# Hard attention over a masked graph: the negated maximum moves from VectorE to GpSimd

## The chip, the cores and the metric

One core of one Trainium2 chip. The metric is the device time of one execution of the whole program in microseconds; the time before is the median of three runs. The profile comes from one further execution with the hardware profiler.

## What is computed

A graph network of four layers over N = 3327 nodes with 256 features and a random adjacency matrix (about 1% of the entries are set). Each layer reads a normalised and rectified x and adds its result to x. The change touches the third layer, the hard attention: eight heads of 32 features, where each node gives one eighth of the value of its best-scoring neighbour. Cut to that layer:

```python
def _L2_gnn_ref(x, adj, WQ, WK, WV, we, be):
    Q = (x @ WQ.T).reshape(n, HEADS, HEAD_DIM).transpose(1, 0, 2)
    K = (x @ WK.T).reshape(n, HEADS, HEAD_DIM).transpose(1, 0, 2)
    V = (x @ WV.T).reshape(n, HEADS, HEAD_DIM).transpose(1, 0, 2)
    energy = Q @ we.T + be
    attn = jnp.einsum('hqd,hkd->hqk', Q, K) * SCALING + energy
    attn = attn + jnp.where(adj > 0, 0.0, -jnp.inf)
    attn = jax.nn.softmax(attn, axis=-1)
    hard = (attn == jnp.max(attn, axis=-1, keepdims=True)).astype(jnp.float32) / HEADS
    out = jnp.einsum('hqk,hkd->hqd', hard, V)
    return out.transpose(1, 0, 2).reshape(n, EMBED)
...
h = jnp.maximum(_layernorm(x, axis=-1), 0.0)
x = x + _L2_gnn_ref(h, adj, L2_gnn_WQ, L2_gnn_WK, L2_gnn_WV, L2_gnn_we, L2_gnn_be)
```

## The kernel before

The nodes are padded to NP = 3328, 26 tiles of 128. The stage in question is `hard_attend` (L1482): for each tile i and each head h it handles one unit g = 8 i + h, 208 in all; below a unit is called a head. The rows of scores are 3328 columns wide and are cut into SCH = 4 steps of SW = 832 columns.

Each engine has its own hand-written queue, and semaphores tie the queues together:

- TensorE computes a step of the scores into one of two PSUM slots (`scores`, L1596, two matmuls of 416 columns), turns the one-hot rows (`transposes_a` L1604, `transposes_b` L1613) and multiplies them with the values (`sums`, L1627, 26 matmuls of 64 columns). Its order is written out: scores of the next heads stand between the transposes and sums of earlier ones. A score step waits until VectorE has finished the step that used its PSUM slot.
- VectorE adds the mask's offset to each step, writes the result S and the step's maximum over the columns to one column of mx (`maxima`, L1699; in the profile this is a custom operation and a short accumulator read). Then `maximum` (L1705) reduces the four columns of mx to their negated maximum nmx. The order is: the steps 1 to 3 of head g, step 0 of head g+1, then `maximum(g)`. S is double, so step 0 of head g waits for the exponential of head g-2 (s_hA) and step 2 for the first GpSimd operation of head g-2 (s_gap).
- ScalarE computes exp(S + nmx) for the first 2048 columns into H (`weights`, L1656), which is one where S is the maximum and zero elsewhere, and copies the transposes of the head before out of PSUM (`evacuate`, L1663 with 1024 and L1665 with 640 columns). Once a tile it takes the result (`take_result`, L1672).
- GpSimd makes the same for the remaining 1280 columns in two operations (`not_hot`): gap = (S + nmx) x a large negative number (L1544), then H = gap clipped to 0 and the code of one (L1549). Beside that it turns the adjacency rows into offsets, in eight pieces of 416 columns a tile (`offsets`, L1538): the table OFF_AT puts two pieces behind each of the heads h = 0, 1, 2 (for the next tile) and h = 7 (for the tile after that). It adds the results to x behind h = 4 and 5 (`add_result`, L1558). At tile 23 it clears rows of the last adjacency buffer once (L1571).

mx and nmx hold two heads each.

Of the kernel before, what the change touches and what calls it, by code (L numbers as in the profile page):

```python
# [17 lines left out]
F32 = mybir.dt.float32  # L18
# [6 lines left out]
ALU = mybir.AluOpType  # L25
ACT = mybir.ActivationFunctionType
AX = mybir.AxisListType

N = 3327
P = 128  # L30
# [1331 lines left out]
SCH = 4  # L1362
# [119 lines left out]
def hard_attend(k, adj_dram, KS, Vhl, be, q_dram):  # L1482


    nc = k.nc
    s_pad, s_nb, s_sc, s_tt, s_mx, s_hA, s_gap, s_hB, s_trA, s_trB, s_evA, s_evB, s_av, s_x, s_res, s_be = (
        k.sem(f"s_h2_{n}") for n in ("pad", "nb", "sc", "tt", "mx", "hA", "gap", "hB", "trA", "trB", "evA", "evB", "av", "x", "res", "be"))
    s_rows = [k.sem(f"s_h2_rows{i}") for i in range(2)]
    s_q = [k.sem(f"s_h2_q{i}") for i in range(2)]
    G = NT * HEADS  # L1490
    CA = TA * 2 * P
    with ExitStack() as c:
# [3 lines left out]
        gap = k.sb(c, "h2_gap", [P, NP - CA], F32)  # L1496
# [2 lines left out]
        HT = k.sb(c, "h2_HT", [P, 2, NP], FP8)  # L1499
        QS = k.sb(c, "h2_QS", [KROWS, 2, HEADS, P], F16)  # L1500
        mx = k.sb(c, "h2_mx", [P, 2, SCH], F32)
        nmx = k.sb(c, "h2_nmx", [P, 2], F32)
        ps = k.ps(c, "h2_ps", [P, 2, 2, CH])
        pT = k.ps(c, "h2_pT", [P, 2, 1024], BF16)
# [3 lines left out]
        @block.sync  # L1508
        def _(sp):
            def load(i):  # L1510
                if i >= 2:
                    sp.wait_ge(s_nb, OFF_PARTS * (i - 1))
                if i < NT - 1:
                    sp.dma_start(rows[:, i % 2, 0:N], adj_dram[i * P:(i + 1) * P, :]).then_inc(s_rows[i % 2], 16)
                else:
                    sp.wait_ge(s_pad, 2)
                    for p0, p1 in LAST_CUTS:
                        sp.dma_start(rows[p0:p1, i % 2, 0:N], adj_dram[i * P + p0:i * P + p1, :]).then_inc(s_rows[i % 2], 16)
                if i >= 2:
                    sp.wait_ge(s_sc, SCH * HEADS * (i - 1))  # L1520
                sp.dma_start(QS[0:3 * HD, i % 2], q_dram[:, :, i * P:(i + 1) * P]).then_inc(s_q[i % 2], 16)

            sp.wait_ge(s_pad, 1)
            for i in range(NT):
                load(i)

        @block.gpsimd
        def _(pool):
            nc.gpsimd.memset(rows[:, :, N:NP], 0).then_inc(s_pad, 1)

            def offsets(i, part):
                c0, c1 = part * NP // OFF_PARTS, (part + 1) * NP // OFF_PARTS
                if part == 0:
                    loads = i // 2 + (1 if i < NT - 1 else len(LAST_CUTS))
                    pool.wait_ge(s_rows[i % 2], 16 * loads)
                    if i >= 2:
                        pool.wait_ge(s_tt, SCH * HEADS * (i - 1))
                nc.gpsimd.tensor_scalar(off[:, i % 2, c0:c1], rows[:, i % 2, c0:c1], -1.0, MASK, ALU.add, ALU.mult).then_inc(s_nb, 1)  # L1538

            def not_hot(g):  # L1540
                pool.wait_ge(s_mx, g + 1)
                if g >= 1:
                    pool.wait_ge(s_hB, g)
                nc.gpsimd.tensor_scalar(gap[:], S[:, g % 2, CA:NP], nmx[:, g % 2:g % 2 + 1], -SHARPER,  # L1544
                                        ALU.add, ALU.mult).then_inc(s_gap, 1)
                pool.wait_ge(s_gap, g + 1)
                if g >= 2:
                    pool.wait_ge(s_trB, g - 1)
                nc.gpsimd.tensor_scalar(H[:, g % 2, CA:NP].bitcast(U8), gap[:], float(FP8_ONE), 0.0,  # L1549
                                        ALU.min, ALU.max).then_inc(s_hB, 1)  # L1550

            def add_result(i, part):
                if part == 0:
                    pool.wait_ge(s_res, i + 1)
                else:
                    pool.wait_ge(s_x, 2 * i + 1)
                xs = k.X[:, i, :].rearrange("p (h d) -> p h d", d=HD)
                nc.gpsimd.tensor_tensor(xs, xs, R[:, :, part, :], ALU.add).then_inc(s_x, 1)  # L1558

            pool.wait_ge(s_pad, 1)  # L1560
            for part in range(OFF_PARTS):
                offsets(0, part)
            offsets(1, 0)
            offsets(1, 1)
            for g in range(G):
                i, h = g // HEADS, g % HEADS
                not_hot(g)
                if i == NT - 3 and h == 0:
                    pool.wait_ge(s_nb, OFF_PARTS * (NT - 2) + 2)
                    pool.wait_ge(s_hB, g + 1)  # L1570
                    nc.gpsimd.memset(rows[96:P, (NT - 1) % 2, :], 0).then_inc(s_pad, 1)  # L1571
                    pool.wait_ge(s_pad, 2)
                if i and h in (ADD_AT, ADD_AT + 1):
                    add_result(i - 1, h - ADD_AT)
                j, parts = OFF_AT[h]
                for part in parts:
                    if 1 <= i + j < NT:
                        offsets(i + j, part)
            add_result(NT - 1, 0)
            add_result(NT - 1, 1)  # L1580
# [103 lines left out]
        @block.vector  # L1684
        def _(dve):
            nc.vector.tensor_copy(QS[3 * HD:KROWS].rearrange("p s h n -> p (s h n)"),
                                  be[3 * HD:KROWS, 3:4].to_broadcast([2, 2 * HEADS * P])).then_inc(s_be, 1)
            two = lambda x: x.rearrange("p (b n) -> p b n", b=2)

            def maxima(g, ch):  # L1690
                i, h = g // HEADS, g % HEADS
                if h == 0 and ch == 0:
                    dve.wait_ge(s_nb, OFF_PARTS * (i + 1))
                if g >= 2 and ch == 0:
                    dve.wait_ge(s_hA, g - 1)
                if g >= 2 and ch == 2:
                    dve.wait_ge(s_gap, g - 1)
                dve.wait_ge(s_sc, g * SCH + ch + 1)
                nc.vector.tensor_tensor_reduce(out=two(S[:, g % 2, ch * SW:(ch + 1) * SW]), in0=ps[:, ch % 2, :, 0:SB],  # L1699
                                               in1=two(off[:, i % 2, ch * SW:(ch + 1) * SW]), scale=SHARP, scalar=-3e38,  # L1700
                                               op0=ALU.add, op1=ALU.max, accum_out=mx[:, g % 2, ch:ch + 1]).then_inc(s_tt, 1)

            def maximum(g):
                dve.wait_ge(s_tt, (g + 1) * SCH)
                nc.vector.tensor_reduce(nmx[:, g % 2:g % 2 + 1], mx[:, g % 2, :], AX.X, ALU.max, negate=True).then_inc(s_mx, 1)  # L1705

            maxima(0, 0)
            for g in range(G):
                for ch in range(1, SCH):
                    maxima(g, ch)  # L1710
                if g + 1 < G:
                    maxima(g + 1, 0)
                maximum(g)


def layer2(k, ap):
    with ExitStack() as c:
        q_dram = k.dram("q_dram", (3 * HD, HEADS, NP), F16)
        KS = k.sb(c, "KS", [KROWS, HEADS, NP], F16)
        be = k.sb(c, "be", [KROWS, 4], F32)  # L1720
        Vhl = k.sb(c, "Vhl", [P, NB2, 2, HEADS, 2 * HD], F16)
        with ExitStack() as c1:
            w = k.sb(c1, "w_hard", [P, 3, 2, KC, D], F16)
            hT = k.sb(c1, "hT2", [P, 2, KC, NP], F16)
            part_of = lambda i: lambda part: w[:, i, part, :, :]
            normalise(k, "n2", hT, [(ap[f"L2_gnn_W{n}"], part_of(i)) for i, n in enumerate("QKV")])
            QT = k.sb(c1, "QT", [P, 2, KC, NP], F16)
            KT = k.sb(c1, "KT", [P, 2, KC, NP], F16)
            hard_project(k, ap, hT, w, QT, KT, KS, Vhl, be, q_dram)
        hard_attend(k, ap["adj"], KS, Vhl, be, q_dram)  # L1730
# [258 lines left out]
```

## Time and profile before

| | |
|---|---|
| median of 3 runs | 2261.28 us (2258.91 to 2265.71) |
| profiled execution | 2261.32 us |
| its span | 2259.6 us |
| VectorE busy over the span | 1891.3 us (84%) |
| TensorE busy over the span | 1995.8 us (88%) |
| ScalarE busy over the span | 1627.9 us (72%) |
| GpSimd busy over the span | 885.3 us (39%) |
| score steps on VectorE (L1699) | 832, 800.0 us, 1021 ns each |
| GpSimd's first operation (L1544) | 208, 277.1 us, 1332 ns each |

The shares over the span are means over very different stages, so they don't say what bounds one of them. The hard attention is read by itself below. PE is TensorE, PEld its weight loads, DVE is VectorE, ACT is ScalarE, POOL is GpSimd. In the rows, `h_S` is the buffer S, `h_nmx` the negated maximum, `h_mx` the four maxima, and so on. Operations on one engine can overlap a little, so the distance from start to start is a better price than the duration.

### The profile page before, as it was taken

The page shows a single profiled execution, that of the slowest core. Times are in us where ns is not written, and L with a number is a line of the kernel's source. Part 1 is how long each engine was busy: PE and PEld are TensorE (multiplying, and loading weights), DVE is VectorE, ACT ScalarE, POOL GpSimd, SP SyncE. Part 2 cuts the span into 40 slices and gives each one's busy share as a digit, 9 for nine tenths or more (in the row PEclk, how much of TensorE's full clock was granted, in tenths as well). Part 3 has the DMA queues.
Part 4 walks back from the last instruction along what each step waited for, and adds up shares of the span by engine and source line. Part 5 has one row for each costly group of instructions (what it writes and reads, how often), then busy time and mean ns, then how long its engine had stood idle before and what let it go on. Part 6 is the DMA issues. An engine that isn't in the chain of part 4 may idle for free. (4 is left out here: it accounts for less than half of the span.)

```text
span 2259.6 us, 58783 instructions
## 1 busy us (share of the span) xinstructions
PE 1995.8 (88%) x23703; PEld 1552.8 (69%) x23703; DVE 1891.3 (84%) x4161; ACT 1627.9 (72%) x1955; POOL 885.3 (39%) x867
## 2 busy tenths in 40 slices
PE   4756999999986799999885999999999999986999
PEld 3546999999984488888643666666666666655544
DVE  5585999999996699988775999999999999985322
ACT  4456999999987576553253999999999999895100
POOL 0020000000000144445233888888888888870000
PEclk9958999999997899999987999999999999997999
DMA  9797121221200356679546111111211111101222
GB/s 314 277 368 314 66 86 66 78 83 60 95 11 6 103 153 170 155 177 200 106 96 183 69 69 63 42 69 69 69 69 67 38 69 69 39 2 52 79 80 69
DMA packets 181870, 240.21 MB, mean 106 GB/s; under 512 B 110484, under 2 KB 148020, under 8 KB 178274
## 3 DMA queue, kind: packets, MB, share of 16 engines
q1 hardware_dynamic: 157201, 208.76, 30.1%
q10 hardware_dynamic: 24400, 27.70, 3.7%
q8 instruction: 188, 3.08, 0.6%
q14 instruction: 81, 0.66, 0.1%
HBM read 160.16 MB, written 47.30 MB: 92 GB/s over the span
## 5 line engine op out<-in xcount | busy, mean ns | idle before, releaser
L1699 DVE CUSTOM_DVE_ANT_0 h_S<-h_ps,h_off 128x832 f32<-128x832 f32 x832 | 800.0, 1021 | 14.2 <-POOL h_off L1538 11.3
L1596 PE MATMUL h_ps<-KS,h_QS 98*128 98x416 f16 x1664 | 441.0, 347 | 81.8 <-DVE h_mx L1699 46.4
L1656 ACT ACTIVATE h_H<-h_S,h_nmx 128x2048 fp8e4<-128x2048 f32 x208 | 416.7, 2003 | 81.3 <-DVE h_nmx L1705 81.3
L834 ACT ACTIVATE b_CA<-b_el,HC 128x1152 fp8e4<-128x1152 f32 (+1 forms) x384 | 435.5, 1219 | 3.5 <-DMA b_el<-el_dram 3.5
L931 PE MATMUL b_pb<-b_x,b_B 128*128 128x132 f16 x5408 | 414.3, 221 | 3.9 <-DVE b_B L896 3.4
L931 PEld LDWEIGHTS b_pb<-b_x,b_B 128*128 128x128 fp8e4 x5408 | 340.3, 96 | 6.7 <-DVE b_B L896 6.2
L1544 POOL TENSOR_SCALAR h_gap<-h_S,h_nmx 128x1280 f32<-128x1280 f32 x208 | 277.1, 1332 | 90.0 <-DVE h_nmx L1705 80.8
L912 PE MATMUL b_pz<-b_x,adjT 128*128 128x134 f16 x2704 | 256.6, 221 | 16.4 <-DMA b_x<-xv_dram 16.4
L1549 POOL TENSOR_SCALAR h_H<-h_gap 128x1280 uint8<-128x1280 f32 x208 | 260.5, 1252 | 17.1
L1627 PEld LDWEIGHTS h_po<-Vhl,h_HT 128*128 128x128 fp8e4 x5408 | 215.1, 98 | 65.0 <-ACT h_HT L1663 0.7
L1596 PEld LDWEIGHTS h_ps<-KS,h_QS 98*128 98x128 f16 x1664 | 95.6, 97 | 199.9 <-DVE h_mx L1699 121.9
L1154 POOL MEMSET c_shift<- 128x1 f32 x1 | 0.1, 98 | 591.4 <-POOLq L963 591.4
L1162 POOL TENSOR_SCALAR c_MK<-c_ad 128x512 f16<-128x512 uint8 x169 | 155.1, 918 | 188.3 <-DVE c_V L1263 142.2
L1627 PE MATMUL h_po<-Vhl,h_HT 128*128 128x64 f16 x5408 | 226.2, 193 | 0.6 <-ACT h_HT L1665 0.6
L1663 ACT ACTIVATE h_HT<-h_pT 128x1024 uint16<-128x1024 uint16 x208 | 209.3, 1006 | 0.2 <-PE h_pT L1604 0.2
L849 DVE TENSOR_SCALAR b_CD<-b_el,HC 128x1152 uint8<-128x1152 f32 (+1 forms) x240 | 195.9, 816 | 8.1 <-DMA b_el<-el_dram 8.1
L912 PEld LDWEIGHTS b_pz<-b_x,adjT 128*128 128x128 fp8e4 x2704 | 183.0, 96 | 16.6 <-DMA b_x<-xv_dram 16.6
L1321 PE MATMUL c_pa<-WHhi,c_V 128*128 128x257 f16 x676 | 185.6, 275 | 0.3 <-DVE c_V L1263 0.2
L1323 PE MATMUL c_pa<-WHhi,c_V 128*128 128x257 f16 x676 | 184.7, 273 | 0.0
L896 DVE TENSOR_TENSOR b_B<-b_CA,adjT 128x288 int32<-128x288 int32 (+1 forms) x384 | 170.2, 470 | 17.2 <-ACT b_CA L834 17.0
L1322 PE MATMUL c_pa<-WHlo,c_V 128*128 128x256 f16 x676 | 184.0, 272 | 0.0
L1892 PE MATMUL m_pa<-m_P,m_ad 128*128 128x512 f16 x676 | 154.4, 380 | 0.3 <-DVE m_P L1924 0.3
(208 smaller groups left out, 3245.4 us busy)
## 6 DMA issues: line engine op xcount, KB each, us to landing
h_rows<-in_adj_dram SPq DMA_DIRECT2D x25, 1663.5 KB, 8.1
b_x<-xv_dram SPq DMA_DIRECT2D x48, 435.5 KB, 5.3
s_rows<-in_adj_dram SPq DMA_DIRECT2D x25, 832.0 KB, 7.1
s_rows<-in_adj_dram SPq DMA_DIRECT2D x25, 831.5 KB, 7.6
e_dram<-c_U ACTq DMA_DIRECT2D x78, 256.0 KB, 2.7
adjT_dram<-adjT SPq DMA_DIRECT2D x1, 10816.0 KB, 38.3
c_ad<-adjT_dram SPq DMA_DIRECT2D x13, 832.0 KB, 6.9
m_ad<-adjT_dram SPq DMA_DIRECT2D x13, 832.0 KB, 4.6
```

The lines of the kernel that those rows point to most:

```text
L834: nc.scalar.activation(dst[:, 0:cols], elr[:, n % 2, 0:cols], ACT.Sigmoid, bias=HC[:, h, 1, jt:jt + 1], scale=STEP, saturate=False).then_i ...
L849: nc.vector.tensor_scalar(dst[:, 0:gn * P].bitcast(U8), elr[:, n % 2, 0:gn * P], HC[:, h, 0, jt:jt + 1], float(FP8_ONE), ALU.is_gt, ALU.mu ...
L912: last = nc.tensor.matmul(pz[:, z % 2, r * WZ:(r + 1) * WZ].rearrange("p (h d) -> p h d", h=2), k.adjT[:, g0 + 3 * b + r, jt, :], xb[:, m ...
L931: last = nc.tensor.matmul(pb[:, p, b, r * W:(r + 1) * W].rearrange("p (f d) -> p f d", f=2), B[:, u % RING_B, t * P:(t + 1) * P], xb[:, m ...
L1321: nc.tensor.matmul(pa[:, q, t, 0:D + 1], hi, WHhi[:, jt, :], start=first, stop=False, skip_group_check=True)
L1544: nc.gpsimd.tensor_scalar(gap[:], S[:, g % 2, CA:NP], nmx[:, g % 2:g % 2 + 1], -SHARPER, ALU.add, ALU.mult).then_inc(s_gap, 1)
L1549: nc.gpsimd.tensor_scalar(H[:, g % 2, CA:NP].bitcast(U8), gap[:], float(FP8_ONE), 0.0, ALU.min, ALU.max).then_inc(s_hB, 1)
L1596: last = nc.tensor.matmul(ps[:, ch % 2, b, 0:SB], QS[:, i % 2, h, :], KS[:, h, c0:c0 + SB], start=True, stop=True)
L1627: last = nc.tensor.matmul(po[:, i % 2, h * 2 * HD:(h + 1) * 2 * HD], wt[:, b, :, e], Vhl[:, b, e, h, :], start=(b == 0 and e == 0), stop=( ...
L1656: nc.scalar.activation(H[:, g % 2, 0:CA], S[:, g % 2, 0:CA], ACT.Exp, bias=nmx[:, g % 2:g % 2 + 1], scale=1.0, saturate=False).then_inc(s_ ...
L1663: nc.scalar.activation(HT[:, g % 2, 0:CA].bitcast(U16), pT[:, 0, :].bitcast(U16), ACT.Copy).then_inc(s_evA, 1)
L1699: nc.vector.tensor_tensor_reduce(out=two(S[:, g % 2, ch * SW:(ch + 1) * SW]), in0=ps[:, ch % 2, :, 0:SB], in1=two(off[:, i % 2, ch * SW:(c ...
```

## The change

The semaphore s_top and a buffer `top` of two columns are added. GpSimd forms the negated maximum in two operations of one column each: `first_maxima` takes the largest of the first three maxima once three steps are done, `maximum` takes the larger of that and the fourth and multiplies by -1. Both stand ahead of `not_hot(g)` in GpSimd's queue. VectorE's queue holds the four steps of each head in plain order and nothing else. All that waited for s_mx (the exponential on ScalarE and the first operation of `not_hot`) now waits for GpSimd's second operation.

```diff
@@ hard_attend
+        top = k.sb(c, "h2_top", [P, 2], F32)
@@ gpsimd
+            def first_maxima(g):
+                q = g % 2
+                pool.wait_ge(s_tt, g * SCH + 3)
+                nc.gpsimd.tensor_scalar(top[:, q:q + 1], mx[:, q, 0:1], mx[:, q, 1:2], mx[:, q, 2:3], ALU.max, ALU.max).then_inc(s_top, 1)
+
+            def maximum(g):
+                q = g % 2
+                pool.wait_ge(s_tt, (g + 1) * SCH)
+                pool.wait_ge(s_top, g + 1)
+                nc.gpsimd.tensor_scalar(nmx[:, q:q + 1], top[:, q:q + 1], mx[:, q, 3:4], -1.0, ALU.max, ALU.mult).then_inc(s_mx, 1)
+
@@
             for g in range(G):
                 i, h = g // HEADS, g % HEADS
+                first_maxima(g)
+                maximum(g)
                 not_hot(g)
@@ vector
-            def maximum(g):
-                dve.wait_ge(s_tt, (g + 1) * SCH)
-                nc.vector.tensor_reduce(nmx[:, g % 2:g % 2 + 1], mx[:, g % 2, :], AX.X, ALU.max, negate=True).then_inc(s_mx, 1)
-
-            maxima(0, 0)
             for g in range(G):
-                for ch in range(1, SCH):
+                for ch in range(SCH):
                     maxima(g, ch)
-                if g + 1 < G:
-                    maxima(g + 1, 0)
-                maximum(g)
```

## Rows read from the trace of the kernel before

**Rows 1.** Busy time by stretch: us, then each engine's busy us (instructions), granted clock, DMA
```profile
core 0: us, PE busy (x) PEld busy (x) DVE busy (x) ACT busy (x) POOL busy (x), PEclk, DMA share, GB/s
...
1320.00:1420.00 100.00, 92.67 (x1227) 62.16 (x1224) 100.00 (x237) 92.28 (x81) 86.28 (x86) 1.00 0.18 62
1420.00:1520.00 100.00, 92.48 (x1224) 62.01 (x1222) 99.87 (x235) 92.36 (x82) 85.88 (x85) 1.00 0.17 59
...
1820.00:1920.00 100.00, 92.67 (x1224) 62.18 (x1224) 100.00 (x236) 92.66 (x83) 85.81 (x85) 1.00 0.17 59
```

**Rows 2.** The reduction's line: count, ns min/median/max, first and last start
```profile
L1705 DVE TENSOR_REDUCE h_nmx<-h_mx x208: 152/154/157, 1227.0 to 2025.2; 128x1 f32<-128x4 f32 x104
```

**Rows 3.** Waits from 1300 to 2010 us: who waited for whom, total, times, longest
```profile
PEld h_ps L1596 <- DVE h_mx L1699: 99.0, 346, 0.4
POOL h_gap L1544 <- DVE h_nmx L1705: 65.5, 96, 1.3
ACT h_H L1656 <- DVE h_nmx L1705: 55.9, 162, 2.1
...
PEld h_pT L1613 <- POOL h_H L1549: 2.0, 1, 2.0
DVE h_S L1699 <- PE h_ps L1596: 1.8, 3, 1.1
```

**Rows 4.** VectorE in order of time: start, us, instruction
```profile
1504.77 1.02 DVE L1699 CUSTOM_DVE_ANT_0 h_S<-h_ps,h_off 128x832 f32<-128x832 f32 x1
...
1505.71 1.02 DVE L1699 CUSTOM_DVE_ANT_0 h_S<-h_ps,h_off 128x832 f32<-128x832 f32 x1
...
1507.60 1.02 DVE L1699 CUSTOM_DVE_ANT_0 h_S<-h_ps,h_off 128x832 f32<-128x832 f32 x1
...
1508.55 0.15 DVE L1705 TENSOR_REDUCE h_nmx<-h_mx 128x1 f32<-128x4 f32 x1
1508.61 1.02 DVE L1699 CUSTOM_DVE_ANT_0 h_S<-h_ps,h_off 128x832 f32<-128x832 f32 x1
```

**Rows 5.** GpSimd in order of time, idle time and releaser in brackets
```profile
1505.11 1.33 POOL L1544 TENSOR_SCALAR h_gap<-h_S,h_nmx 128x1280 f32<-128x1280 f32 x1
1506.52 1.25 POOL L1549 TENSOR_SCALAR h_H<-h_gap 128x1280 uint8<-128x1280 f32 x1
1507.86 1.16 POOL L1538 TENSOR_SCALAR h_off<-h_rows 128x416 f32<-128x416 int32 x2
1509.11 1.33 POOL L1544 TENSOR_SCALAR h_gap<-h_S,h_nmx 128x1280 f32<-128x1280 f32 x1
...
1520.32 1.33 POOL L1544 TENSOR_SCALAR h_gap<-h_S,h_nmx 128x1280 f32<-128x1280 f32 x1 [0.56 <-DVE h_nmx L1705]
1521.74 1.25 POOL L1549 TENSOR_SCALAR h_H<-h_gap 128x1280 uint8<-128x1280 f32 x1
1522.95 0.73 POOL L1558 TENSOR_TENSOR X<-X,h_R 128x256 f32<-128x256 f32 x1
1524.17 1.33 POOL L1544 TENSOR_SCALAR h_gap<-h_S,h_nmx 128x1280 f32<-128x1280 f32 x1 [0.49 <-DVE h_nmx L1705]
```

**Rows 6.** GpSimd's groups by shape: count, busy us, mean ns, idle before
```profile
L1544 POOL TENSOR_SCALAR h_gap<-h_S,h_nmx 128x1280 f32<-128x1280 f32 x208 | 277.1, 1332 | 90.0 <-DVE h_nmx L1705 80.8 <-POOL h_H L1549 0.2
L1549 POOL TENSOR_SCALAR h_H<-h_gap 128x1280 uint8<-128x1280 f32 x208 | 260.5, 1252 | 17.1
...
L1538 POOL TENSOR_SCALAR h_off<-h_rows 128x416 f32<-128x416 int32 x208 | 111.8, 537 | 24.5 <-DMA h_rows<-in_adj_dram 8.1
...
L372 POOL TENSOR_SCALAR_AFFINE_SELECT s_corner_f<-s_ones_pp 128x128 f32<-128x128 f32 x1 | 0.3, 283 | 0.3 <-POOL s_rows L369 0.3
...
L1154 POOL MEMSET c_shift<- 128x1 f32 x1 | 0.1, 98 | 591.4 <-POOLq L963 591.4
```

**Rows 7.** GpSimd at the start of the stage, eight offset pieces in a row
```profile
1217.16 4.85 POOL L1538 TENSOR_SCALAR h_off<-h_rows 128x416 f32<-128x416 int32 x8 [7.56 <-DMA h_rows<-in_adj_dram]
```

**Rows 8.** ScalarE's exponential in order of time, idle before it in brackets
```profile
1504.89 2.00 ACT L1656 ACTIVATE h_H<-h_S,h_nmx 128x2048 fp8e4<-128x2048 f32 x1 [0.34 <-DVE h_nmx L1705]
```

**Rows 9.** TensorE: two windows with granted clock, and score matmuls at either clock
```profile
660.00:670.00 10.00, 7.42 (x107) 6.00 (x105) 10.00 (x26) 9.99 (x11) 0.00 (x0) 1.00 0.00 0
...
1225.00:1230.00 5.00, 4.35 (x10) 0.65 (x10) 4.98 (x12) 2.00 (x1) 2.58 (x2) 0.50 0.53 226
...
1218.31 0.14 PEld L1596 LDWEIGHTS h_ps<-KS,h_QS 98*128 98x128 f16 x2 [18.90 <-issue]
...
1231.68 0.90 PE L1596 MATMUL h_ps<-KS,h_QS 98*128 98x416 f16 x2
...
1504.85 0.53 PE L1596 MATMUL h_ps<-KS,h_QS 98*128 98x416 f16 x2
```

More of the change, by code:

```diff
@@ L1485, in hard_attend @@
     nc = k.nc
-    s_pad, s_nb, s_sc, s_tt, s_mx, s_hA, s_gap, s_hB, s_trA, s_trB, s_evA, s_evB, s_av, s_x, s_res, s_be = (
-        k.sem(f"s_h2_{n}") for n in ("pad", "nb", "sc", "tt", "mx", "hA", "gap", "hB", "trA", "trB", "evA", "evB", "av", "x", "res", "be"))
+    s_pad, s_nb, s_sc, s_tt, s_mx, s_hA, s_gap, s_hB, s_trA, s_trB, s_evA, s_evB, s_av, s_x, s_res, s_be, s_top = (
+        k.sem(f"s_h2_{n}") for n in ("pad", "nb", "sc", "tt", "mx", "hA", "gap", "hB", "trA", "trB", "evA", "evB", "av", "x", "res", "be", "top"))
     s_rows = [k.sem(f"s_h2_rows{i}") for i in range(2)]
```

## The prediction

> **What bounds the kernel now.** I began with the busy time by stretch [rows 1]. Between 1320 and 1920 us the kernel does one thing, the hard attention, and there VectorE is busy 99.9 to 100% of the time, TensorE 92%, ScalarE 92% and GpSimd 86%. The reader should see two things: VectorE has no air, and GpSimd has only 14%. The stage is long: the reduction that the change removes runs 208 times, once for each head of each of 26 tiles, from 1227.0 to 2025.2 us [rows 2], 35% of the span.
>
> Next come the waits of the stage [rows 3]. VectorE waited 1.8 us for TensorE in 710 us; everybody else waits for VectorE. TensorE waits for the maxima in 346 cases (weight loads), ScalarE's exponential waits 55.9 us for the negated maximum, GpSimd's first operation 65.5 us. So VectorE's queue sets the pace.
>
> VectorE's instructions in order of time [rows 4] give that pace. Steps start at 1504.77 and 1505.71, 0.94 us apart, although each lasts 1.02 (they overlap). Only the step behind the reduction starts later: the reduction starts at 1508.55 with the end of the step of 1507.60, and the next step at 1508.61, 1.01 behind its predecessor. One head is 1508.61 - 1504.77 = 3.84 us, a tile of eight heads 30.74 (26 of them are 799 us).
>
> GpSimd's instructions in order of time [rows 5] are the view that decides this case. A head with two pieces of the offset runs gap 1505.11, H 1506.52, two pieces from 1507.86, next gap 1509.11: 4.00 us without idle time, more than VectorE's 3.84. Four heads of a tile are like this (h = 7, 0, 1, 2), and GpSimd falls behind in them; it catches up in the others, where gap waits 0.56 or 0.49 us for the maximum. Being late harms nobody now, since ScalarE gets the maximum from VectorE.
>
> **Part 1, what leaves VectorE.** The reduction lasts 0.154 us [rows 2], but overlaps the next step; what it costs is 1.01 - 0.94 = 0.067 us a head [rows 4]. With VectorE alone the head would take 3.777 us, a tile 30.22, and 208 heads would save 208 x 0.067 = 14 us. That is all the change can win at the bound. The new order also gives the maximum of a head without waiting for the next head's first step, up to 0.94 us earlier; this shortens a latency once, at the start of the stage, not the pace.
>
> **Part 2, what arrives at GpSimd.** Per head two single-column operations. The first waits for the third step, the second for the fourth step and for the first; gap waits for the second, and behind it in GpSimd's queue stand H, the offset pieces and the residual additions, then the next head. ScalarE's exponential now waits for GpSimd too, so GpSimd's lateness becomes everybody's.
>
> GpSimd's own work per tile before [rows 5]: 4 offset heads x 4.00 = 16.00. A plain head is 1.41 (gap to H) + 1.25 (H) + 0.08 (the distance that GpSimd keeps behind an operation) = 2.74, twice 5.48. A head with an addition runs 1520.32 to 1522.95 + 0.73 = 3.36, plus 0.08, twice 6.88. Sum 28.36 of 30.74. So the two new operations have 30.74 - 28.36 = 2.38 us a tile, 0.30 a head, before the kernel gets slower than now, and 0.23 a head (30.22 - 28.36 = 1.86 by 8) to give the full gain.
>
> Price of the two, called x; no row has one-column arithmetic on GpSimd, so I bound it by neighbours [rows 6]. H (1280 columns, constants alone) lasts 1252 ns, the offset piece (416 columns) 537: 0.83 ns a column, which leaves 0.19 us that doesn't depend on the width. Gap, 1280 columns too but with one operand out of a column of the memory, lasts 1332, so 0.27 fixed. The eight pieces in a row [rows 7] take 4.85 us, so (4.85 - 0.54) / 7 = 0.62 each, 0.08 behind the end of the former; gap to H, which waits for gap, has the same 0.08. Both new operations have such column operands and a successor that waits for them: 0.27 + 0.08 = 0.35 each, **x = 0.70 us**. Above: the first reads two such columns; at 0.08 each that makes 0.78, and with 0.08 for the extra waits 0.86. Below: the 128-column select (283 ns, some 0.175 fixed at 0.83 a column) gives 2 x 0.255 = 0.51; the one-column memset, which reads nothing, 2 x (0.098 + 0.08) = 0.36. Memset is the end of the range, since the new operations read and compute. I take 0.70, as gap is the same instruction with the same kind of operand.
>
> The Trainium skill says in "GPSIMD Engine Reference", section 2.1 Instruction dispatch, that finding and calling the routine costs "one indirect call (tens of cycles) per instruction". If that were all that a one-column operation costs, x would be under the 0.23 and the sum would be that of the second case below; the fixed 0.19 to 0.27 us of the rows speak against it, and I follow the rows.
>
> **The sum.** With x = 0.70 a tile is 28.36 + 8 x 0.70 = 33.96 us of GpSimd work against VectorE's 30.22, so GpSimd becomes the bound: +3.22 us against 30.74. Tiles 0 to 23: 24 x 3.22 = 77.3. Tile 24 has one pair of pieces fewer (-1.25): +2.0. The last tile has none, 28.36 - 5.0 + 5.6 = 28.96, so VectorE sets 30.22 there: -0.5. GpSimd's one long memset (2.9 us) is on GpSimd's path now and mostly was before, where TensorE waited 2.0 us for H right there [rows 3]: +0.4. The earlier first maximum: -0.9 + 0.35. Together +79 us. The profiled execution took 2261.3 us, 1.7 more than its span of 2259.6 and equal to the median of the runs (2261.28): 2261.3 + 79 = **2340 us**.
>
> Does anything else end later than GpSimd? Heads without pieces need 2.74 + 0.70 = 3.44 or 4.14 us, and a run of four of them 15.2, 3.79 a head, against VectorE's 3.777; and VectorE may run two heads ahead, as its buffers are double. From one maximum, the exponential (2.0) frees the buffer for four steps (3.78): 6.2 us for two heads, 3.1 a head. ScalarE has 3.5 a head, since it idles 0.34 of 3.84 [rows 8]. All of them hide under 4.25. The 0.067 us that VectorE is spared are then worth nothing.
>
> **The rivals.**
> (a) GpSimd becomes the bound: 2340. By x: 0.36 gives 2272, 0.51 gives 2302, 0.78 gives 2356, 0.86 gives 2372 (25 tiles x 8 x the difference). For it: the 86% in rows 1 and the 4.00 us head. Chance 0.85.
> (b) The other side: one-column operations cost GpSimd little, both together under 0.23 us, VectorE stays the bound and its 0.067 us come home: 2261 - 14 = 2247. It decides at 0.30 us a head, 0.15 for each operation. For it: the memset's 98 ns. Against: each new operation waits for one before it and is waited for, so no overlap. Chance 0.07.
> (c) x between these, about 0.25 to 0.33, and gain and loss cancel: 2255 to 2268. Chance 0.05.
> (d) TensorE idles more and loses its clock. It would be busy 92% x 3.84 / 4.25 = 84%. Its clock stayed at 2.4 GHz (1.00 granted) at 7.42 busy of 10 us, and was at 1.2 (0.50) at the start of the stage, after idle time of 18.9 us [rows 9]. A fall each tile for some 10 us, at 1.7 times the TensorE time of a head (0.90 against 0.53 us for a pair of score matmuls), would cost 10 x (1 - 4.25/6.0) = 3 us, 26 times: 2415. Chance 0.03.
> The Trainium skill's "TensorE: Matmul & The Clock Gate", section "A second HAM failure mode: psum-queue depth-cycling", describes a clock that swings where the engine idles briefly between groups of matmuls; by this rule (d) would hold, and the present stage, with such idling in front of its scores, shows 1.00 throughout, which speaks against it.
>
> **How the numbers follow.** The forecast is (a). The bound of 0.3%, 6.8 us, is about what a measurement of this kernel can tell from no change. (b) is faster, (c) mostly the same, (a) and (d) slower: 0.07, 0.05, 0.88. The range takes x from its lower bound of 0.36 (2272, a little below for (c)) to 0.86 (2372) and something for imperfect overlap, were the four quick heads not to catch up: 4 x 4.70 + 2 x 4.14 + 2 x 3.78 = 34.6 instead of 33.96, +17 us. So 2266 to 2380, with (b), (d) and the far end of (a) outside.
>
> **What would show it.** Right: GpSimd at 98 to 100% occupied counting its 0.08 gaps, in the windows of the stage; a head of 4.7 us with pieces and near 3.4 without; ScalarE's exponential waiting about 0.75 us a head on GpSimd; VectorE waiting for the exponential or for gap; VectorE's steps 0.94 apart with no step at 1.01. Wrong: if the one-column operations start under 0.15 us apart, or if VectorE stays at 100%, (b) holds. A granted clock under 0.95 in the stage means (d). If the offset heads are 4.7 but the others 3.8, the catching up failed and the time is some 17 us higher.

## The result: slower by 5.0%

The changed kernel took 2375.07 us (median of four runs, 2374.51 to 2378.21), against 2262.74 us for the kernel before on the same chip: a ratio of 1.0505, 95% interval 1.0487 to 1.0523, that is +112 us. The profiled execution has a span of 2372.8 us, 113.2 more than before. The forecast was 2340 us, with a range of 2266 to 2380. The direction and the mechanism hold; the loss is 112 us where 79 were expected, and the rows and experiments below show in which term.

### The profile page after: what moved, and what is told of

Its sections match the earlier page's. It is cut to its first block and busy times, and to the rows that moved or that the text cites. A ratio compares the mean times of both kernels' runs of the same rounds, so it can differ in the third digit from the quotient of the medians.

```text
span 2372.8 us, 59199 instructions
## 1 busy us (share of the span) xinstructions
PE 1995.0 (84%) x23703; PEld 1552.8 (65%) x23703; DVE 1902.9 (80%) x3953; ACT 1628.1 (69%) x1955; POOL 1020.3 (43%) x1283
## 5 line engine op out<-in xcount | busy, mean ns | idle before, releaser
L1713 DVE CUSTOM_DVE_ANT_0 h_S<-h_ps,h_off 128x832 f32<-128x832 f32 x832 | 809.3, 1022 | 115.8 <-ACT h_H L1670 69.1
L1610 PE MATMUL h_ps<-KS,h_QS 98*128 98x416 f16 x1664 | 450.0, 353 | 68.6 <-DVE h_mx L1713 27.7
L1556 POOL TENSOR_SCALAR h_gap<-h_S,h_nmx 128x1280 f32<-128x1280 f32 x208 | 277.1, 1332 | 19.4
L1561 POOL TENSOR_SCALAR h_H<-h_gap 128x1280 uint8<-128x1280 f32 x208 | 260.5, 1252 | 18.2
L1618 PE MATMUL h_pT<-ident,h_H 128*128 128x128 bf16 x1664 | 130.1, 222 | 135.2 <-ACT h_HT L1677 135.2
L1618 PEld LDWEIGHTS h_pT<-ident,h_H 128*128 128x128 bf16 x1664 | 100.7, 98 | 206.7 <-issue 202.6
L1610 PEld LDWEIGHTS h_ps<-KS,h_QS 98*128 98x128 f16 x1664 | 109.0, 100 | 137.7 <-DVE h_mx L1713 94.0
```

The lines of the kernel that those rows point to most:

```text
L1610: last = nc.tensor.matmul(ps[:, ch % 2, b, 0:SB], QS[:, i % 2, h, :], KS[:, h, c0:c0 + SB], start=True, stop=True)
L1618: last = nc.tensor.transpose(pT[:, 0, b * P:(b + 1) * P], H[:, g % 2, b * 2 * P:(b + 1) * 2 * P].bitcast(BF16), k.ident16[:])
```

## The profile after

Busy time by stretch, the changed kernel, as in [rows 1] (a stretch of 600 us in the middle of the stage, and one of 10 us in it, which is taken up further below):

```profile
core 0: us, PE busy (x) PEld busy (x) DVE busy (x) ACT busy (x) POOL busy (x), PEclk, DMA share, GB/s
1320.00:1920.00 600.00, 477.49 (x6361) 321.07 (x6361) 529.41 (x1085) 481.39 (x425) 534.42 (x712) 0.98 0.16 56
...
1410.00:1420.00 10.00, 8.25 (x94) 5.67 (x94) 8.07 (x17) 7.14 (x7) 8.76 (x14) 0.83 0.01 2
```

VectorE fell from 100% to 88%, TensorE from 93 to 80%, ScalarE from 92 to 80%, and only GpSimd rose, from 86 to 89%. GpSimd at 89% doesn't look like a bound. That the stage runs at its pace is seen in its queue instead:

```profile
1502.89 0.36 POOL L1544 TENSOR_SCALAR h_top<-h_mx 128x1 f32<-128x1 f32 x1
...
1507.83 0.36 POOL L1544 TENSOR_SCALAR h_top<-h_mx 128x1 f32<-128x1 f32 x1
1508.36 0.30 POOL L1550 TENSOR_SCALAR h_nmx<-h_top,h_mx 128x1 f32<-128x1 f32 x1 [0.17 <-DVE h_mx L1713]
1508.75 1.33 POOL L1556 TENSOR_SCALAR h_gap<-h_S,h_nmx 128x1280 f32<-128x1280 f32 x1
1510.17 1.25 POOL L1561 TENSOR_SCALAR h_H<-h_gap 128x1280 uint8<-128x1280 f32 x1
1511.51 1.15 POOL L1539 TENSOR_SCALAR h_off<-h_rows 128x416 f32<-128x416 int32 x2
1512.77 0.36 POOL L1544 TENSOR_SCALAR h_top<-h_mx 128x1 f32<-128x1 f32 x1
...
1523.56 1.33 POOL L1556 TENSOR_SCALAR h_gap<-h_S,h_nmx 128x1280 f32<-128x1280 f32 x1
1524.98 1.25 POOL L1561 TENSOR_SCALAR h_H<-h_gap 128x1280 uint8<-128x1280 f32 x1
1526.21 0.36 POOL L1544 TENSOR_SCALAR h_top<-h_mx 128x1 f32<-128x1 f32 x1
...
1527.13 1.33 POOL L1556 TENSOR_SCALAR h_gap<-h_S,h_nmx 128x1280 f32<-128x1280 f32 x1
...
1531.40 1.34 POOL L1556 TENSOR_SCALAR h_gap<-h_S,h_nmx 128x1280 f32<-128x1280 f32 x1
...
1538.34 0.36 POOL L1544 TENSOR_SCALAR h_top<-h_mx 128x1 f32<-128x1 f32 x1
```

Every operation follows the last at 0 to 0.17 us. A head with offset pieces is 1512.77 - 1507.83 = 4.94 us (4.00 before, [rows 5]), a plain one 1527.13 - 1523.56 = 3.57 (2.74 of work before), one with an addition 1531.40 - 1527.13 = 4.27 (3.44). A tile, from the first row to the last, is 35.45 us against 30.74. The last maximum of the stage started at 2139.2 us after 1226.3 for the first; before it was 2025.2 after 1227.0 [rows 2]: 912.9 in place of 798.2, 114.7 us more. That is the whole difference of the spans, less 1.5 us at the ends.

```profile
L1550 POOL TENSOR_SCALAR h_nmx<-h_top,h_mx x208: 296/297/299, 1226.3 to 2139.2; 128x1 f32<-128x1 f32 x104
```

The waits of the stage from 1300 to 2010 us, to lay beside [rows 3]:

```profile
ACT h_H L1670 <- POOL h_nmx L1550: 140.2, 121, 1.4
PE h_pT L1618 <- ACT h_HT L1677: 109.1, 131, 1.3
...
DVE h_S L1713 <- ACT h_H L1670: 56.3, 74, 0.8
POOL h_nmx L1550 <- POOL h_top L1544: 21.4, 127, 0.2
...
DVE h_S L1713 <- PE h_ps L1610: 15.1, 56, 0.9
```

The chain has turned round. Before, GpSimd waited 65.5 us for VectorE, and VectorE 1.8 for anyone. Now ScalarE waits 140 us for the maximum from GpSimd, VectorE 56 us for ScalarE's exponential and 15 for scores. No row of GpSimd waiting for another engine is among the large ones.

And GpSimd's groups by shape (count, busy us, mean ns, idle before):

```profile
L1544 POOL TENSOR_SCALAR h_top<-h_mx 128x1 f32<-128x1 f32 x208 | 74.7, 359 | 12.1 <-DVE h_mx L1713 1.6
L1550 POOL TENSOR_SCALAR h_nmx<-h_top,h_mx 128x1 f32<-128x1 f32 x208 | 61.7, 297 | 36.0 <-POOL h_top L1544 27.3 <-DVE h_mx L1713 8.7
```

An operation of one column lasts 0.36 us when both of its scalar operands are columns, and 0.30 when one is a column and the other a constant.

## The experiments

Two theories. **A, load:** GpSimd's queue is the bound, and every operation in it counts with its distance to the next, whoever reads it. **B, chain:** what costs is that the exponential waits for GpSimd; the new operations hurt by their place in the chain from VectorE over GpSimd to ScalarE. The waits above can be read either way.

**The load alone, without the chain.** The kernel before, reduction kept, plus two operations that nobody reads:

```diff
@@ gpsimd
+            def load_alone(g):
+                q = g % 2
+                pool.wait_ge(s_tt, g * SCH + 3)
+                nc.gpsimd.tensor_scalar(top[:, q:q + 1], col[:, 0:1], col[:, 1:2], col[:, 2:3], ALU.max, ALU.max).then_inc(s_top, 1)
+                pool.wait_ge(s_tt, (g + 1) * SCH)
+                pool.wait_ge(s_top, g + 2)
+                nc.gpsimd.tensor_scalar(low[:, q:q + 1], top[:, q:q + 1], col[:, 3:4], -1.0, ALU.max, ALU.mult)
...
+            nc.gpsimd.memset(col[:], 1.0).then_inc(s_top, 1)
+            pool.wait_ge(s_top, 1)
@@
+                load_alone(g)
                 not_hot(g)
```

> The kernel before, with VectorE's reduction kept and all waits on it kept, plus the same two single-column operations at the same place in GpSimd's queue, reading constants and read by nobody. Only GpSimd's load is added, ScalarE doesn't wait for it. Theory A (load): GpSimd has 35.5 us a tile against VectorE's 30.74, and since VectorE's third step waits for gap of two heads before, the time is 2365 to 2378 again. Theory B (chain through ScalarE): 2262, since nobody waits for the added operations.

2370.38 us, ratio 1.0491 (1.0476 to 1.0507), against 1.0505 of the change (1.0487 to 1.0523): the two can't be told apart. Theory A. ScalarE again waits, but for VectorE, since VectorE itself is held; the brake now shows as waits for H:

```profile
PEld h_pT L1627 <- POOL h_H L1560: 197.8, 153, 2.2
ACT h_H L1670 <- DVE h_nmx L1719: 137.1, 159, 2.6
PE h_pT L1627 <- POOL h_H L1560: 130.8, 117, 1.8
DVE h_S L1713 <- PE h_ps L1610: 79.2, 98, 1.6
```

GpSimd's first operation of a head and the same one a tile later, 35.28 us apart:

```profile
1500.89 1.33 POOL L1555 TENSOR_SCALAR h_gap<-h_S,h_nmx 128x1280 f32<-128x1280 f32 x1
...
1536.17 1.33 POOL L1555 TENSOR_SCALAR h_gap<-h_S,h_nmx 128x1280 f32<-128x1280 f32 x1
```

The scores of a step stand behind the transposes of H in TensorE's queue, so a late GpSimd stops VectorE this way just as well. Without the chain from GpSimd's maximum to the exponential, and with the load alone, 111 us are still there. Theory B isn't needed for any part of the 112 that these runs can tell.

**The other work taken out of GpSimd's queue.** The changed kernel without the offset pieces of the tiles 2 to 25:

```diff
@@ sync
-                    sp.wait_ge(s_nb, OFF_PARTS * (i - 1))
+                    sp.wait_ge(s_tt, SCH * HEADS * (i - 1))
@@ gpsimd
-                    if 1 <= i + j < NT:
+                    if i + j < 2:
                         offsets(i + j, part)
@@ vector
-                    dve.wait_ge(s_nb, OFF_PARTS * (i + 1))
+                    dve.wait_ge(s_nb, OFF_PARTS * min(i + 1, 2))
```

The adjacency rows are still loaded; their buffer is now freed by VectorE's steps. Three waits that keep the loads in order, at the memset and at the end of GpSimd's queue, are left out of the excerpt.

> The changed kernel with the offset pieces of the tiles 2 to 25 left out (the mask of tile 0 or 1 is used again, so the output is not the reference's). GpSimd has 28.2 - 5.0 + 7.4 = 30.5 us a tile against VectorE's 30.2. Theory A (GpSimd's load): 26 x 30.5 in place of 35.5, 2375 - 25 x 5.0 = 2250 (2246 to 2258). Theory B (chain): the pieces are not in the chain from a maximum to the exponential, so little changes, over 2340.

2251.06 us, ratio 0.9962 (0.9948 to 0.9976) to the kernel before: the loss of 112 us became a gain of 8. The chain is untouched and is still there, and costs at most the 5 to 7 us by which this run stays above the one with a single operation and no pieces, which follows below. The same was taken out of the kernel before:

> The kernel before, with the offset pieces of the tiles 2 to 25 left out as in the run on the changed kernel (the output is not the reference's). GpSimd falls from 28.2 to 23.2 us a tile, VectorE stays at 30.74. Theory A: VectorE is the bound of the kernel before, and GpSimd's work is worth nothing there; 2257 to 2260, at most 2.5 us less for the one stall that GpSimd's memset causes. Theory B (GpSimd's long heads of 4.0 us already cost something before the change): under 2250.

2259.96 us, ratio 0.9996 (0.9984 to 1.0007). So 5 us a tile of GpSimd's work are worth nothing before the change and 120 us after it. That says which engine bounds which kernel.

**One operation in place of two.**

```diff
-                first_maxima(g)
                 maximum(g)
@@
-                pool.wait_ge(s_top, g + 1)
-                nc.gpsimd.tensor_scalar(nmx[:, q:q + 1], top[:, q:q + 1], mx[:, q, 3:4], -1.0, ALU.max, ALU.mult).then_inc(s_mx, 1)
+                nc.gpsimd.tensor_scalar(nmx[:, q:q + 1], mx[:, q, 2:3], mx[:, q, 3:4], -1e30, ALU.max, ALU.min).then_inc(s_mx, 1)
```

> The changed kernel with one single-column operation a head on GpSimd in place of two: the first is left out, and the second makes a constant from two of the maxima, so the maximum is not computed and the output is not the reference's. Theory A (GpSimd's queue is the bound and each operation counts with its start-to-start distance): before the change GpSimd has 28.2 us a tile, the one operation costs 0.38 to 0.40, so 31.3 us a tile against 35.5 with two; the time is 2261 + 25 x 0.6 = 2272 to 2280. Theory B (what costs is the chain, maximum on GpSimd and then the exponential on ScalarE, whose start is late however short the operation): the chain only gets 0.5 us shorter of several, and the time stays over 2320.

2284.84 us, ratio 1.0111 (1.0096 to 1.0127), +25.5 us where 12 to 20 were expected. It lies 5 us above the range of theory A and 35 below that of theory B. The rest is in the rows:

```profile
1504.76 0.28 POOL L1549 TENSOR_SCALAR h_nmx<-h_mx 128x1 f32<-128x1 f32 x1 [0.35 <-DVE h_mx L1711]
...
1509.14 0.28 POOL L1549 TENSOR_SCALAR h_nmx<-h_mx 128x1 f32<-128x1 f32 x1
...
1536.52 0.28 POOL L1549 TENSOR_SCALAR h_nmx<-h_mx 128x1 f32<-128x1 f32 x1 [0.35 <-DVE h_mx L1711]
```

A tile is 31.76 us. Once in it the operation stands 0.35 us behind the one before it, where it stands 0.09 behind without a wait, so 0.26 us are waiting and 31.5 work: I had started from 28.2 us for the work before and should have used the 28.36 of the prediction. The 0.26 us are lost because the heads without pieces (3.14 us of work when plain) run out of maxima: near balance, GpSimd is the bound in some of the heads and VectorE in others, and two buffers don't level that out completely. 25 x (31.76 - 30.74) = 25.5.

**One operation and no offset pieces,** so that VectorE is the bound for certain:

> The changed kernel with one single-column operation a head in place of two (no true maximum) and without the offset pieces of the tiles 2 to 25; the output is not the reference's. GpSimd has about 26.2 us a tile, so VectorE is the bound for certain and its steps have no reduction between them. Theory A: the full gain of the removal, 208 x 0.067 = 14 us, shows up: 2243 to 2248. Rival: the reduction's 0.067 us would be filled by something else on VectorE (its waits for the exponential): 2255 to 2260.

2245.95 us, ratio 0.9931 (0.9914 to 0.9948), -14.5 us (12 to 19 by the interval), and 14.0 less than the kernel before without its pieces. This is the gain that the change was able to bring. VectorE's steps, in this run and in the kernel before (count, ns min/median/max, first and last start):

```profile
L1713 DVE CUSTOM_DVE_ANT_0 h_S<-h_ps,h_off x832: 1018/1019/1025, 1220.1 to 2008.1; 128x832 f32<-128x832 f32 x167
```

```profile
L1699 DVE CUSTOM_DVE_ANT_0 h_S<-h_ps,h_off x832: 1015/1022/1026, 1222.1 to 2024.1; 128x832 f32<-128x832 f32 x167
```

The first and the last start are 788.0 us apart against 802.0, 14.0 = 208 x 0.067 less. In the run without pieces but with both operations they are 792.1 apart, and there VectorE waited 4.6 us, 2.2 of them at one time for the exponential.

**The second wait.** In the changed kernel the second operation stands 0.17 us behind the first. It waits for two semaphores, so one wait was moved to the first operation:

```diff
@@ first_maxima
-                pool.wait_ge(s_tt, g * SCH + 3)
+                pool.wait_ge(s_tt, (g + 1) * SCH)
@@ maximum
-                pool.wait_ge(s_tt, (g + 1) * SCH)
                 pool.wait_ge(s_top, g + 1)
```

> The changed kernel with the wait for the fourth step moved from the second operation to the first, so that the second has one semaphore wait in place of two. It stood 0.17 us behind the end of the first, where other operations on GpSimd stand 0.08 behind. Theory C (the second wait costs a slot of the sequencer): the gap falls to 0.08 and the time by 208 x 0.08 = 16 us to 2359. Theory D (it is the way of a semaphore back to an engine whose queue has nothing to cover it, after so short an operation): the gap stays and so does the time, 2375.

2363.1 us, ratio 1.0458 (1.0443 to 1.0474) against 1.0505 (1.0487 to 1.0523). The second operation now comes 0.46 us behind the start of the first, 0.53 before:

```profile
1499.77 0.36 POOL L1544 TENSOR_SCALAR h_top<-h_mx 128x1 f32<-128x1 f32 x1 [0.23 <-DVE h_mx L1712]
...
1504.63 0.36 POOL L1544 TENSOR_SCALAR h_top<-h_mx 128x1 f32<-128x1 f32 x1
1505.09 0.30 POOL L1549 TENSOR_SCALAR h_nmx<-h_top,h_mx 128x1 f32<-128x1 f32 x1
1505.48 1.34 POOL L1555 TENSOR_SCALAR h_gap<-h_S,h_nmx 128x1280 f32<-128x1280 f32 x1
```

That is theory C's direction: the gap fell from 0.17 to 0.10 us (0.08 expected), and the time with it. 208 x 0.07 = 15 us would follow, 11 to 12 were measured; part of the rest is that the first operation now sometimes waits for the fourth step, as in the row of 1499.77. The semaphore that was moved had been reached before the first of the two operations even started in 196 of the 208 heads of the changed kernel, and the gap was 0.17 there too. But this is no price of every second wait: gap waits for two semaphores as well, and so does H, and each stands only 0.09 us behind the operation before it (1508.75 and 1510.17 in the changed kernel). What sets this pair apart is not shown.

**A full kernel with one operation.** VectorE's third and fourth steps start from the maxima of the first and second, so that one operation on GpSimd is enough:

```diff
@@ gpsimd
-                first_maxima(g)
                 maximum(g)
@@
-                pool.wait_ge(s_top, g + 1)
-                nc.gpsimd.tensor_scalar(nmx[:, q:q + 1], top[:, q:q + 1], mx[:, q, 3:4], -1.0, ALU.max, ALU.mult).then_inc(s_mx, 1)
+                nc.gpsimd.tensor_scalar(nmx[:, q:q + 1], mx[:, q, 2:3], mx[:, q, 3:4], -1.0, ALU.max, ALU.mult).then_inc(s_mx, 1)
@@ vector
+                if ch >= 2:
+                    dve.wait_ge(s_tt, g * SCH + ch - 1)
@@
-                                               in1=..., scale=SHARP, scalar=-3e38,
+                                               in1=..., scale=SHARP,
+                                               scalar=(mx[:, g % 2, ch - 2:ch - 1] if ch >= 2 else -3e38),
```

> A full kernel that needs one single-column operation: VectorE's third step starts its maximum from that of the first step, the fourth from that of the second (an operand out of mx in place of a constant), so the larger of the last two is the row's maximum, and GpSimd forms it in one operation. If the operand costs VectorE nothing, this is the run with one operation again, 2280 to 2288. If it breaks the overlap of VectorE's steps (0.94 us apart, 1.02 long), two steps of each head start 0.1 us or more later, 208 x 0.2 = 40 us more at VectorE, and it takes 2300 or over.

2297.58 us, ratio 1.0161 (1.0142 to 1.0180). Between the two cases: the overlap of the steps doesn't break, but it shrinks.

```profile
1504.74 1.08 DVE L1713 CUSTOM_DVE_ANT_0 h_S<-h_ps,h_off,h_mx 128x832 f32<-128x832 f32 x1
...
1505.75 1.02 DVE L1713 CUSTOM_DVE_ANT_0 h_S<-h_ps,h_off 128x832 f32<-128x832 f32 x1
...
1506.69 1.02 DVE L1713 CUSTOM_DVE_ANT_0 h_S<-h_ps,h_off 128x832 f32<-128x832 f32 x1
...
1507.64 1.08 DVE L1713 CUSTOM_DVE_ANT_0 h_S<-h_ps,h_off,h_mx 128x832 f32<-128x832 f32 x1
...
1508.64 1.08 DVE L1713 CUSTOM_DVE_ANT_0 h_S<-h_ps,h_off,h_mx 128x832 f32<-128x832 f32 x1
```

```profile
1513.72 0.29 POOL L1549 TENSOR_SCALAR h_nmx<-h_mx 128x1 f32<-128x1 f32 x1 [0.61 <-DVE h_mx L1713]
...
1545.81 0.29 POOL L1549 TENSOR_SCALAR h_nmx<-h_mx 128x1 f32<-128x1 f32 x1 [0.61 <-DVE h_mx L1713]
```

A step that takes its start value from a column lasts 1.08 in place of 1.02, and the next one starts 1.00 to 1.01 behind it, not 0.94. Two of them cost some 0.12 us a head, nearly twice what the reduction costs, so VectorE's head of 1508.64 - 1504.74 = 3.90 us is longer than the 3.84 of the kernel before. Each of the two steps also has one wait more than before, and the run doesn't part that from the operand; the longer duration points to the operand. VectorE now needs 31.2 us a tile and GpSimd some 31.6, and with both so near each other a tile takes 32.09. The version is 78 us quicker than the change as it was made, but what it spares GpSimd it pays at VectorE in part, and it stays slower than the kernel before.

**Relieving GpSimd.** Two runs tried to make room for the operations, and a third looked for the reason why the first was slow. The first gave 128 of its columns to ScalarE, on top of the paired maxima; GpSimd clips in the other sense there, so that ScalarE can copy the transposes without inverting them.

```diff
+    CE = CA + 128
-                nc.gpsimd.tensor_scalar(gap[:], S[:, g % 2, CA:NP], nmx[:, g % 2:g % 2 + 1], -SHARPER,
+                nc.gpsimd.tensor_scalar(gap[:], S[:, g % 2, CE:NP], nmx[:, g % 2:g % 2 + 1], SHARPER,
-                                        ALU.min, ALU.max).then_inc(s_hB, 1)
+                                        ALU.add, ALU.max).then_inc(s_hB, 1)
@@ scalar
...
-                nc.scalar.activation(H[:, g % 2, 0:CA], S[:, g % 2, 0:CA], ACT.Exp, ...
+                nc.scalar.activation(H[:, g % 2, 0:CE], S[:, g % 2, 0:CE], ACT.Exp, ...
```

> The kernel with paired maxima, and 128 of GpSimd's 1280 columns given to ScalarE's exponential (2176 columns). GpSimd clips in the other sense (56 + gap, at least 0), so that its half needs no inversion afterwards. GpSimd saves 2 x 128 x 0.83 ns = 0.21 us a head: 31.2 - 1.7 = 29.5 us a tile, ScalarE gets 0.11 to 0.12 on its 3.5. Theory A: VectorE is the bound again without its reduction, 30.2 us a tile: 2246 to 2254, under the kernel before. Rival: the long heads (4.2 us) and ScalarE's later start don't average out within two buffers, and 10 us or so stay: 2255 to 2270.

2849.68 us, ratio 1.2600 (1.2576 to 1.2624). Neither case; GpSimd's second pass had become slow. TensorE's granted clock is low in this run too (0.76 and 0.70 from 1400 to 1600 us), but GpSimd is busy 95% there and waits for nobody, so its queue is the bound. Two more runs: the other clip alone in the changed kernel,

```diff
-                nc.gpsimd.tensor_scalar(gap[:], S[:, g % 2, CA:NP], nmx[:, g % 2:g % 2 + 1], -SHARPER,
+                nc.gpsimd.tensor_scalar(gap[:], S[:, g % 2, CA:NP], nmx[:, g % 2:g % 2 + 1], SHARPER,
...
-                                        ALU.min, ALU.max).then_inc(s_hB, 1)
+                                        ALU.add, ALU.max).then_inc(s_hB, 1)
```

and a single pass that compares with the maximum:

```diff
-                nc.gpsimd.tensor_scalar(gap[:], S[:, g % 2, CA:NP], nmx[:, g % 2:g % 2 + 1], -SHARPER,
-                                        ALU.add, ALU.mult).then_inc(s_gap, 1)
...
-                nc.gpsimd.tensor_scalar(H[:, g % 2, CA:NP].bitcast(U8), gap[:], float(FP8_ONE), 0.0,
-                                        ALU.min, ALU.max).then_inc(s_hB, 1)
+                nc.gpsimd.tensor_scalar(H[:, g % 2, CA:NP].bitcast(U8), S[:, g % 2, CA:NP], nmx[:, g % 2:g % 2 + 1], 0.0,
+                                        ALU.add, ALU.is_ge).then_inc(s_hB, 1)
```

> The changed kernel with GpSimd's second pass in the other sense only: (gap + 56, at least 0) in place of (gap, at most 56, at least 0), written as bytes as before, and a plain copy on ScalarE. It tells what made the run with 128 columns shifted slow. If it is the pair of operations add and max with bytes written: the pass takes 1280 x 3.56 = 4.6 us and the time is near 2261 + 208 x (4.6 - 1.25) - 15 + 114 = 3040. If it was the shift itself (start column or length): the pass stays at 1.25 us and the time at 2375.

> The changed kernel with both single-column operations, but GpSimd makes its 1280 columns in one pass in place of two: H = (S + negated maximum >= 0), one or zero as bytes, and ScalarE multiplies by the code of one where it copies the transposes out. Theory A (GpSimd's load is all that makes the change slow): if this pass runs at the 0.83 ns a column of the others, GpSimd loses 1.33 us a head, 35.5 - 10.6 = 24.9 us a tile, VectorE is the bound at 30.2 and the time is 2243 to 2250. If the pass runs at the 3.56 ns a column that adding and clipping to bytes took in the run before (4.1 us for 1152 columns), it takes 4.6 us in place of 2.74 and the time goes to 2750. Theory B (the chain from GpSimd to ScalarE is what costs): with a quick pass still over 2300.

3075.2 us (one run; 3040 expected, though its terms add up to 3057) and 2791.11 us, ratio 1.2343 (1.2326 to 1.2359; 2750 expected for a slow pass). The three passes, by shape, in this order: the shifted kernel, the other clip, the single pass:

```profile
L1561 POOL TENSOR_SCALAR h_H<-h_gap 128x1152 uint8<-128x1152 f32 x208 | 853.0, 4101 | 18.2
```

```profile
L1561 POOL TENSOR_SCALAR h_H<-h_gap 128x1280 uint8<-128x1280 f32 x208 | 953.3, 4583 | 18.2
```

```profile
L1558 POOL TENSOR_SCALAR h_H<-h_S,h_nmx 128x1280 uint8<-128x1280 f32 x208 | 967.3, 4651 | 19.4
```

min and max with bytes written take 1252 ns for 1280 columns [rows 6], add and max 4583, add and a comparison 4651: 3.7 times as long for the same shape and types. The other clip is slow without any shift, so the shift was not the reason; but moving 128 columns with the quick pair was not tried, and the single pass didn't test theory B either. What both give is theory A at a much larger load. The other clip adds 4.58 - 1.25 = 3.33 us a head to the change: 208 x 3.33 + 112 = 805 us expected, 815 measured. The single pass adds 3.40 and drops gap with its distance, 1.42: 208 x 1.98 + 112 = 524 expected, 531 measured.

No version that computes the whole layer beats the kernel before. The runs that beat it (2251 and 2246 us) leave the offsets out, and the second of them the maximum too.

## Why the prediction was right, and where it was off

- *VectorE bounds the stage before, GpSimd has 0.30 us a head to spare.* Right: taking away 5 us a tile of GpSimd's work changed nothing in the kernel before, and a single operation of about 0.38 us already made it 1.1% slower.
- *What leaves VectorE is worth 0.067 us a head, 14 us.* Right: 14.5 us, between 12 and 19, when nothing else bounds.
- *GpSimd becomes the bound; its own work is 28.36 us a tile.* Right, shown by the load alone (111 of 112 us). 28.36 + 8 x 0.887 is the 35.45 that a tile takes.
- *x = 0.70 us for the two operations.* This is the term that was mis-sized; it measured 0.89. In a head with pieces the difference to before is 0.94, in the others 0.83. The rows give 0.53 from the first operation to the second and 0.39 from there to gap, 0.92; behind H or an addition without pieces the first one comes without the 0.08 (1526.21 is the end of H), so 0.83 there. Set against the two times 0.35 of the prediction, the first operation is 0.09 longer (0.36 for 0.27), its gap 0.09 longer (0.17 for 0.08, of which the run with a single wait takes back 0.07), the second 0.03 longer (0.297 for 0.27). I had named the first two as the upper bound, 0.86, and then taken the lower figure since gap is the nearest row. Gap has one column operand where the first has two, and stands 0.09 behind the operation before it although it too waits for two semaphores, so that row could not show the 0.17.
- *The size.* 25 tiles x 8 x 0.19 = 38 us too little, against 33 found. Some of the rest is in the first tile, which takes 34.0 us against 31.8 before, 2.3 more, where nearly every later one takes 4.7 more; the other 2 to 3 us stay open. The measured x is above the upper bound of 0.86, at which rival (a) gives 2372. That 2375 still lies in the range is luck: it is in the 8 us left for quick heads that don't catch up, and they did catch up.
- *Everything else hides.* Right: heads of 3.57 and 4.27 us follow each other without GpSimd waiting for a maximum, and the 22 tiles between the first and the one with the memset take 35.40 to 35.44 us each from gap to gap. VectorE's waits (88% busy) are the consequence, since the load alone brings the same time. ScalarE waited for GpSimd 140.2 us in 710, 0.88 us a head where 0.75 were expected.
- *The clock.* TensorE's share fell to 80%, and the granted clock was 0.98 of 2.4 GHz on average from 1320 to 1920 us, so rival (d) with its sign of less than 0.95 didn't happen. Short falls did: 0.83 from 1410 to 1420 us, for one, so part of it at the lower level of 1.2 GHz, where TensorE was busy 8.25 of 10 us. They cost nothing that shows: the tile in which this one lies took 35.42 us, like its neighbours.
- *The sign of 98 to 100% for GpSimd* was meant with the gaps, and so it came true: 534.4 us busy and 712 gaps of 0.08 make 591 of 600 us, 98.6%. Whoever looks at the share alone, 89% beside VectorE's 88%, would not take GpSimd for the bound.

## What to carry to other kernels

An engine's room is the period of the bound minus its work counted from start to start, here 0.30 us a head at 86% busy; compare what is moved to it with that, not with its idle share. A one-column operation took 0.53 and 0.39 us from start to start on GpSimd, as much as some 640 and 470 columns more in a long pass (0.83 ns each), while VectorE hid all but 0.067 us of its reduction behind the next step. To find which engine bounds, add work that nobody reads, and take out work that shares only the queue: here both gave the answer without touching the chain.

## What was not expected of the hardware

- GpSimd's tensor-scalar with float in and bytes out took 1252 ns for 1280 columns with min and max, and 4583 with add and max, 4651 with add and a comparison. Other pairs in this kernel are quick (add and multiply with float out: 1332). Why is open.
- VectorE's reducing step lasted 1.08 in place of 1.02 us, and the next started 0.06 us later, when its start value came from a column of the memory; that is nearly what the whole reduction of four columns cost before, which overlaps the next step.
- A second semaphore wait on the second one-column operation on GpSimd cost 0.07 us although it had been reached before the operation ahead of it started in 196 of 208 heads, while gap and H, with two waits each, stand 0.09 us behind the operation before them. Why is open.
- Behind H or an addition the first one-column operation started with no gap at all (1526.21), behind the offset pieces 0.11 us later (1512.77). Why is open.
